# Letting the attention stage start inside the projection stage, with its first pass in two halves around the fold

## The reference

```python
def _L0_xattn_ref(q, k, v, Wq, bq, Wk, bk, Wv, bv, interference, amp, Wo, bo):
    ...
    def proj(x, W, bias):
        y = x @ W.T + bias
        y = y.reshape(b, s, H, dk, M)
        return jnp.transpose(y, (0, 2, 1, 3, 4))
    ...
    def interfere(x):
        return x + 0.1 * amp[0] * jnp.einsum('bhsdi,hij->bhsdj', x, interference)
    qh, kh, vh = (interfere(qh), interfere(kh), interfere(vh))
    scores = jnp.einsum('bhqdm,bhkdm->bhqkm', qh, kh) / math.sqrt(dk)
    weights = jax.nn.softmax(scores, axis=3)
    out = jnp.einsum('bhqkm,bhkdm->bhqdm', weights, vh)
    out = jnp.transpose(out, (0, 2, 1, 3, 4)).reshape(b, s, dm)
    return out @ Wo.T + bo
...
x = x + jnp.tanh(g_xattn[0]) * _L0_xattn_ref(_layernorm(x, axis=-1), ctx_4096, ctx_4096, ...)
x = x + jnp.tanh(g_ffn[0]) * _L0_ffn_ref(_layernorm(x, axis=-1), ...)
return x
```

## Time and profile before

| | |
|---|---|
| median of 3 runs | 1482.92 us (lowest 1480.61, highest 2315.33) |
| the profiled execution, its own time | 1477.51 us |
| its span in the trace | 1475.7 us |
| instructions | 22268 |
| TensorE busy | 1394.1 us, 94% of the span |
| VectorE, ScalarE, GpSimd busy | 673.8, 396.8, 234.3 us |
| mean granted TensorE clock | 0.972 |
| projections | until about 612 us of the span |
| attention | from 619.5 us to about 1070 us |
| feed-forward | from 1075.7 us to the end |

### The profile page before, as it was taken

One profiled execution on the slowest core, in us unless ns is written; L12 is line 12 of the kernel. 1 busy time (PEld: TensorE's weight loads), 2 busy tenths in 40 slices (PEclk: granted clock), 3 DMA queues, 4 the chain that ended last, 5 costly groups with the idle time before them and its releaser, 6 DMA issues. The chain is left out here.

```text
span 1475.7 us, 22268 instructions
## 1 busy us (share of the span) xinstructions
PE 1394.1 (94%) x8592; PEld 1153.3 (78%) x8592; DVE 673.8 (46%) x1377; ACT 396.8 (27%) x736; POOL 234.3 (16%) x400
## 2 busy tenths in 40 slices
PE   7999999999999999669999999999968999999998
PEld 6887887878888888457777777777756888888887
DVE  5322131231655544456666767676656424333211
ACT  3311111011212212224555555455424111110100
POOL 0000000000000000014555555555600000000000
PEclk9999999999999999858999999999979999999999
DMA  5763645536457777866777776776451211211101
GB/s 195 204 173 129 142 147 136 146 135 145 162 164 182 167 191 187 249 177 191 209 224 208 224 227 209 215 202 201 133 219 43 90 68 58 86 43 72 57 29 57
DMA packets 181719, 224.86 MB, mean 152 GB/s; under 512 B 24048, under 2 KB 122352, under 8 KB 181616
## 3 DMA queue, kind: packets, MB, share of 16 engines
q1 hardware_dynamic: 167792, 189.90, 44.3%
q10 hardware_dynamic: 13824, 33.56, 7.1%
HBM read 136.89 MB, written 85.46 MB: 151 GB/s over the span
## 5 line engine op out<-in xcount | busy, mean ns | idle before, releaser
L963 DVE TRANSPOSE_TENSOR_REDUCE part<-bank 128x16 f32<-128x512 f32 x256 | 167.7, 693 | 28.9 <-PE bank L837 26.8
L916 ACT ACTIVATE probT<-bank 128x512 f32<-128x512 f32 x256 | 138.6, 595 | 128.3 <-PE bank L868 128.3
L151 PE MATMUL bank<-place_a,w_hi 128*128 128x512 f32 x384 | 152.1, 396 | 7.9 <-DVE place_a L144 7.9
L495 DVE SCALAR_TENSOR_TENSOR stage_lo<-bank,bias_mixed,stage_hi 128x512 fp32r<-128x512 f32 x64 | 48.0, 751 | 240.1 <-ACT stage_hi L497 240.1
L153 PE MATMUL bank<-place_a,w_lo 128*128 128x512 f32 x384 | 150.5, 392 | 0.0
L152 PE MATMUL bank<-place_a,w_hi 128*128 128x512 f32 x384 | 150.0, 391 | 0.0
L497 ACT ACTIVATE stage_hi<-bank,bias_mixed 128x512 fp32r<-128x512 f32 x64 | 44.0, 688 | 268.1 <-PE bank L153 259.3
L816 PE MATMUL bank<-place_a,oT_hi 128*128 128x512 f32 x256 | 108.1, 422 | 0.3 <-POOL oT_lo L1042 0.3
L1236 DVE SCALAR_TENSOR_TENSOR v_place<-bank,gates,v_place 128x512 f32<-128x512 f32 x32 | 24.0, 751 | 175.1 <-PE bank L153 175.1
L151 PE MATMUL bank<-place_a,yT_hi 128*128 128x512 f32 x256 | 102.1, 399 | 1.5 <-DVE place_c L144 1.5
L151 PE MATMUL bank<-place_b,place_a 128*128 128x512 f32 x256 | 100.4, 392 | 1.4 <-DVE place_c L144 1.4
(11 more groups left out here) (179 smaller groups left out, 2698.4 us busy)
## 6 DMA issues: line engine op xcount, KB each, us to landing
q_in<-q_rows SPq DMA_DIRECT2D x212, 100.0 KB
k_in<-k_rows SPq DMA_DIRECT2D x84, 196.0 KB
k_rows<-stage_hi SPq DMA_DIRECT2D x128, 128.0 KB, 2.5
v_pad<-v_out SPq DMA_DIRECT2D x32, 512.0 KB, 2.7
q_rows<-stage_hi SPq DMA_DIRECT2D x128, 128.0 KB, 2.5
v_place<-v_pad ACTq DMA_DIRECT2D x32, 512.0 KB, 4.7
v_place<-x_mid SPq DMA_DIRECT2D x30, 512.0 KB, 3.6
k_rows<-stage_lo SPq DMA_DIRECT2D x64, 128.0 KB, 2.5
```

The source lines that it names most:

```text
L151: nc.tensor.matmul(bank_ap, sh, mh, start=(i == 0), stop=False)
L495: lambda bank: nc.vector.scalar_tensor_tensor(out=lo[:], in0=bank[:], scalar=bias, in1=hi[:].bitcast(F32), op0=ALU.add, op1=ALU.subtract),
L916: act.activation(probT[o % NPT][:, i].rearrange("k a p q -> k (a p q)"), two_bank[i][:], ACT.Exp).then_inc(s_exp, 1)
L963: dve.tensor_reduce(part[at][:, :, 2 * i:2 * i + 2, :].rearrange("k a p b -> k a (p b)"), one_bank[i][:].rearrange("k (a b t) -> k a b t", ...
```

## The change

The change has four parts.

- **One program part.** Projections and attention share one `nc.Block()`. Each engine goes on from its last projection job to its first attention slot without a barrier. `projected(eng)` makes SyncE and ScalarE wait at the start of their attention code for all projection jobs and all stores. TensorE waits for the bank that it is about to use; the banks' roles are numbered anew (`turn`), and the second half of a first pass gets the bank of the last query job.
- **Four octets loaded early.** Octets 0 to 3 get buffers of their own place in SBUF (`early_q`, `early_k`, where `mix`, `bv_row` and `v_out` lay) and are loaded during the last four query jobs. Two output-weight chunks now follow each of the query jobs 1 and 2, so that none is left at the end.
- **First pass in two halves.** `first_pass(o, 1)` fills the second bank, which no fold uses, and stands at the start of slot o. `first_pass(o, 0)` fills the first bank and stands at the end of slot o. The fold of octet s moves from slot s to slot s + 1, in the middle of the slot's work, and with it the maxima of octet s and GpSimd's two instructions. The second pass of octet s - 3 stands at the beginning of slot s, or right after the values and the fold.
- **SyncE.** In a slot `load_oct` now comes before `place_max`. The loads of the feed-forward's first x tiles are issued at other slots and wait for other semaphores.

```diff
-        with proj, ExitStack() as st, nc.Block() as block:
+        attend = top.enter_context(ExitStack())
+        block = attend.enter_context(nc.Block())
+        with proj, ExitStack() as st:
...
-                    elif c:
-                        wo_chunk(c - 1, free_places)
+                    elif 0 < c < KC - 1:
+                        for _ in range(2 if c < 3 else 1):
+                            wo_chunk(wo_next, free_places)
+                            wo_next += 1
...
+                    if g == NG - 1 and c >= KC - EARLY:
+
+                        def load_early(sp, o=c - (KC - EARLY)):
+                            sp.wait_ge(s_cleared, EARLY)
+                            sp.wait_ge(s_stage[o % 2], 96 * ((NG * KC + o) // 2 + 1))
+                            load_kq(sp, o, (first_k, second_k, early_k[2], early_k[3])[o],
+                                    early_q[o] if o else first_q, s_kq[o])
+                        plan.append((len(line.jobs) + 0.7, load_early))
...
+            def projected(eng):
+
+                eng.wait_ge(project_line.emptied, len(project_line.jobs))
                 for i in range(2):
-                    sp.wait_ge(s_stage[i], 96 * NG * KC)
-                    sp.wait_ge(s_vst[i], 16 * NB)
-            run_phase(block, line, plan, stores_end)
+                    eng.wait_ge(s_stage[i], 96 * NG * KC)
+                    eng.wait_ge(s_vst[i], 16 * NB)
...
-                for o in range(1, LAG):
-                    load_oct(o)
+                projected(sp)
                 for s in range(SLOTS):
+                    if EARLY <= s + LAG < OCTS:
+                        load_oct(s + LAG)
                     if 1 <= s <= OCTS:
                         place_max(s - 1)
-                    if s + LAG < OCTS:
-                        load_oct(s + LAG)
...
+                def first_pass(o, i):
+                    if o < OCTS:
+                        slot = o % KQ
+                        if i == 1:
+                            pe.wait_ge(s_kq[slot], 48 * (o // KQ + 1))
+                            if o:
+                                pe.wait_ge(s_part, 2 * o - 1)
+                        elif o:
+                            pe.wait_ge(s_max, o)
+                        if o == 0:
+                            pe.wait_ge(project_line.emptied, project_line.last_use(turn[i]))
+                        for p in (2 * i, 2 * i + 1):
+                            dst = one_bank[i][:].rearrange("k (a p q) -> k a p q", a=2, p=2)[:, :, p % 2, :]
+                            last = pe.matmul(dst, k_in[slot][:, p, :], q_in[slot][:, :, p, :], start=True, stop=True,
+                                             skip_group_check=True)
+                        last.then_inc(s_one, 1)
...
+                for s in range(SLOTS):
+                    work, h = proj_at(s), half_at(s, 0)
+                    first_pass(s, 1)
+                    if h is not None:
+                        values(h)
+                        fold(s - 1)
+                        second_pass(s - LAG)
+                    else:
+                        second_pass(s - LAG)
+                        for part_of in work[:1]:
+                            project(*part_of)
+                        fold(s - 1)
+                    for part_of in work[1:]:
                         project(*part_of)
+                    first_pass(s, 0)
```

More of the change, by code:

```diff
@@ L35, in bank, with last_use @@
         return self.banks[n % len(self.banks)]
+    def last_use(self, i):
+        return max(n for n, job in enumerate(self.jobs) if job.pe and n % len(self.banks) == i) + 1
     def wait_filled(self, eng, end):
@@ L167, in build @@
         first_k, second_k = (sb(n, [ROWS, 4, P], F32R) for n in ("first_k", "second_k"))
-        KQ = 6
+        with ExitStack() as overlaid:
+            mix = sb("mix", [P, KC, P], stack=overlaid)
+            bv_row = sb("bv_row", [P, D], stack=overlaid)
+            v_out = [sb(f"v_out{i}", [P, PAIRS // 2, 2, 32], F32, overlaid) for i in range(2)]
+        with ExitStack() as overlaid:
+            yin, raw_d = ([sb(f"{n}{i}", [P, D], F32, overlaid)[:] for i in range(2)] for n in ("yin", "raw_d"))
+        early_q = {i: sb(f"early_q{i}", [ROWS, 2, 4, P], F32R) for i in (2, 3, 1)}
+        early_k = {i: sb(f"early_k{i}", [ROWS, 4, P], F32R) for i in (2, 3)}
+        KQ, EARLY = 6, 4
         s_kq = [sem(f"s_kq{i}") for i in range(KQ)]
@@ L684, in build @@
         wo_hi, wo_lo = place_a, place_c
         dn_hi, dn_lo = (half_place(place_b, i, NE * R) for i in range(2))
-        v_place = [sb(f"v_place{i}", [P, 2 * D]) for i in range(2)]
         with ExitStack() as overlaid:
@@ L712, in build @@
             gated = sb("gated", [P, HALF], F32, st)
-            one_bank, two_bank, v_bank, o_bank = (banks[2 * i:2 * i + 2] for i in range(4))
+            turn = [(len(project_line.jobs) - 2 + i) % len(banks) for i in range(len(banks))]
+            one_bank, two_bank, v_bank, o_bank = ([banks[i] for i in turn[2 * j:2 * j + 2]] for j in range(4))
             norm = LayerNorm("c", st)
@@ L1001, in _ @@
                             stages[s - start](dve)
+                    if s < OCTS:
+                        partial_max(s, 0)
             @block.gpsimd
             def _(pool):
-                for i in range(2, KQ, 2):
-                    pool.memset(q_in[i][:].bitcast(F32), 0.0).then_inc(s_zero[0], 1)
+                project_line.wait_filled(pool, len(project_line.jobs))
+                for i in range(EARLY, KQ):
+                    pool.memset(q_in[i][:].bitcast(F32), 0.0).then_inc(s_zero[i % 2], 1)
                 def add_gated(b, out):
```

142 lines of the change are left out of this document (62 added, 80 removed).

## The result

The changed kernel takes a median of 1604.6 us (1597.95 to 1608.27 in 4 runs). Its ratio to the kernel before is 1.0824, with an interval of 1.0762 to 1.0886: 8% slower. Two of the four runs of the kernel before on that chip (2315.33 and 2784.32 us) lie far above the other two (1480.61 and 1482.92 us) and are left out of the ratio.

A forecast was written before the change was run, and what follows sets the result against it. The steady attention was taken as bound by TensorE (busy 303.74 of 313 us). From 1477.5 us: -4 at the junction, +65 and +1.6 for gaps, +44 for the clock, giving 1584 us; range 1505 to 1640.

The forecast's parts named there:

- case (C): The forecast itself: a gap in every steady period plus low clock after it, 1584 us; chance 0.42.
- the two value slots at the start: Value slots before product triples begin: give some 1.5 us of the junction's gain back through late maxima.
- The start of the attention: Junction: SyncE let go at about 623, first second pass near 632, a gain of 5.5 us.
- The junction's net: Junction gain less what the first two value slots give back: -4 us, bounds +1 and -12.
- The gap: Steady slots: TensorE waits 3.0 us a period for maxima two slots after the values; +65 us over 26 periods.
- Their 8 KB travel on the same queue as the 400 KB loads, and they land after the load ahead of them: SyncE's queue in the slots: maxima land after the load ahead of them, taken as 0.3 us behind it.
- The clock: Steady slots: 85 in 100 gaps bring a low-clock stretch costing 2.0 us; 1.7 us a period, +44 us.
- Rival B: Steady slots: the gap comes but the clock holds, giving 1540 us; chance 0.33.
- The period: Steady slots: TensorE's work 12.45 us, plus 3.0 of gap and 1.7 of clock, instead of 12.97.
- The exponentials' wait: Slot after a value slot: the second pass's second half waits 0.35 us for the exponentials, its cover gone.
- Rival A: Slots: maxima overtake the load, so no gap and no waits for keys; 1456 us, 1.5% faster; chance 0.12.
- The end of the attention and the feed-forward part: After the last first passes: x tiles loaded later still land in time, feed-forward untouched; no change in time.

The follow-up runs named there:

- e5: The junction's part of the change alone, on the kernel before: slots as before, maxima placed ahead of the load; 1472.17 us, ratio 0.9955.
- e2: The kernel before with SyncE's two steps exchanged, the load issued before the maxima; 1540.58 us, ratio 1.0414.
- e1: The changed kernel with SyncE's two steps in the old order, maxima placed before the load; 1509.49 us, ratio 1.0207 to the kernel before.
- e6: The changed kernel without the v tile loads after the first four, leaving out part of the computation; 1518.82 us, ratio 1.0275 to the kernel before.
- e4: The changed kernel with the maxima's DMA issued by GpSimd on its own queue; 1585.3 us, ratio 1.0716 to the kernel before.
- e3: The changed kernel with 13 filler matmuls of zeros before the late second pass; 1564.82 us, ratio 1.0577 to the kernel before.
- e8: e7 with a value slot's fold moved to between the two halves of the values; 1458.99 us, ratio 0.9862 to the kernel before.
- e7: e5 with a value slot's second pass ahead of the values and ScalarE's exponentials before its copy; 1466.74 us, ratio 0.9927 to the kernel before.

## Why the prediction came out as it did

The forecast, 1584 us and slower by more than 2%, named the right case (C) with the right mechanism of the gap and the clock; the measured 1604.6 lies in its range, 20 us above it. The step that failed is the sum's term for the two value slots at the start, put at 1.5 us where the trace has 7.1. By its steps:

- **The start of the attention.** Forecast: `projected` lets SyncE go at about 623 and the first second pass starts near 632. The trace: 621.44 (the bias row's issue) and 631.79. e5, which has the maxima first, gains 8.0 us at that point and 6.4 at the end, by the medians.
- **"The two value slots before the product triples begin give some 1.5 us back".** This is the term that was mis-sized: from octet 0 to octet 13 the changed kernel loses 7.1 us on the kernel before. The two gaps alone take 3.62 and 4.31 us, in the rows of 655.51 and 673.00, longer than the steady ones. The forecast's own sum would have given that: without the two triples of 0.69 us in TensorE's work, 7.25 - (4.07 - 1.38) = 4.6 us a gap, an estimate from its terms. The granted clock was low, too, for 27 us instead of 14 between 650 and 690. e2 loses 6.8 us in the same piece from the load-first order alone, and e1, without that order, 2.1. The junction's net was forecast at -4 us and came to +1.4 at octet 13.
- **The gap.** Forecast: 3.0 us once a period, in the slot two after the values, ended by the DMA of the maxima. The trace: 26 gaps there (octets 14 to 114), 2.1 to 4.1 us long, 3.06 in the mean. Its parts fit as well: from the load's issue to the second pass 6.62 us in the mean, forecast 6.10 + 0.3 + 0.1 = 6.5; between the two second passes 7.39, forecast 7.25; and TensorE's work in it 4.3, forecast 4.07. e1 and e2 show that SyncE's order makes the gap, and e6 that the v tile makes 2.2 us of the delay. One size was off: the last two periods, forecast at 1.6 us together because no v tile is loaded in them, had gaps of 1.4 and 2.7 us and cost 6.4 us.
- **"Their 8 KB travel on the same queue as the 400 KB loads, and they land after the load ahead of them".** The second half held; the reason that the first half suggests did not. In a value slot they land with the load on GpSimd's queue all the same (e4).
- **The clock.** Forecast: 85 in 100 gaps bring on a low stretch that costs 2.0 us, 44 us in all. The trace: 25 of the 26 gaps have a low stretch beside them, 21 of 3.4 us and four of 6.8 us, 99 us in all, of which half is lost: 49 us. So the share was too low and the price right. e3 gives back 40 us with the delay kept, some of it eaten by the filler. Rival B is refuted as a forecast; its price of 1540 lies 25 us under the 1565 of e3, whose clock held. Its argument, the gap of 1.84 us before 231 that did no harm, was weak: in the changed kernel's trace the gap at that same place (1.83 us, before 228) was followed by a low stretch, from 229.4, and the one before 139 was not.
- **The period.** Forecast: 12.45 + 3.0 + 1.7 = 17.15 us. Over the 26 periods it covers it was 17.44 (octet 13 to 117; before 12.97), of which 3.06 are gap and 1.90 clock; the 12.48 left bear out the 12.45, though the recorded parts of that number (up to 0.25 us gained, 0.35 of wait) don't add up to it. That the 17.19 of the table is so near to 17.15 is luck: it takes in the shorter periods at the end. The 26 periods lost 116.3 us against 65 + 44 = 109.
- **The exponentials' wait** of 0.35 us is there, a little smaller: the second pass of the slot after the values takes 0.90 us (908.82) instead of 0.63. The first passes wait for no keys, as forecast, and VectorE costs nothing in the steady slots.
- **Rival A** falls: in a value slot, with a load in flight, the maxima are waited for until 6 us after their issue and not 2.6. e8 comes near its price of 1456 with 1459, but by another order of the slots. Its premise that with the maxima in time the rest follows doesn't hold for this order: e1 has late loads and late maxima at once. I made the same mistake once more in what I expected of e1.
- **The end of the attention and the feed-forward part** lost 2.6 us, forecast as nothing; no run looked into it.

Together: 5.4 us at the junction, 7.3 in the 26 periods, 4.8 in the last two and 2.6 behind them are the 20 us by which the forecast was low.

The change, then, is a junction worth 6 us, a new order of TensorE's slots that costs 26 to 37, and an order of two DMAs that costs 95 of which some 40 are clock. What stays open: how the 26 to 37 us split up beyond the 15 us of waits for DMAs and the 7 of the exponentials, and whether the fold or the moved second pass makes them; and why the packets of a small DMA start late beside a large one of another queue.

## What to carry to other kernels

Where a small transfer that the next step waits for shares the DMA engines with a prefetch, count from the event that lets the prefetch go to the use of the small one, with the prefetch's full time in between, and count it in each slot that is short, the first ones too; here another queue for the small one did not save it. Issue the small one first, and free the prefetch's buffers earlier (e7 and e8) rather than let the prefetch overtake. In this kernel a TensorE gap of 3.1 us in every period cost 1.9 us more by the clock behind it, and gaps of about 1 us cost next to nothing more (e6), so shortening such a gap pays more than its own length. And where a mean per period comes out as forecast, look at the periods one by one before you call the forecast right.

## What the runs showed that was not expected

- **The price of the clock can be read inside one trace.** In e4 the gaps before 774.30 and 789.67 (1.7 and 2.7 us) brought no low stretch, and the periods that follow them take 15.4 and 15.0 us. From 805 to 1112, where each gap has one, a period takes 17.1 us in the mean.
- **Low stretches come evenly.** In the changed kernel's trace they begin at 690.2, 707.3, 724.4, 741.4, 758.5 and so on up to 1072.5, at distances of 17.07 us and twice 20.5, while single periods there take 16.3 to 19.1 us. There is one for each gap, and the mean distance (17.38 us) is the mean period of that piece (17.40), so the evenness doesn't show that gaps and clock keep step; why the distances are so equal was not tried.
- **Shorter gaps in every period left the clock nearly alone**: from 690 to 1100 three low stretches in e6 (waits of 1.1 us in the mean) and one in e1 (0.7 us), eleven in e2 (1.5 us), where 3 us brought one in nearly every period. The same length does not always do the same: in e4 2.65 us brought none (before 789.67) and 2.55 us one (before 821.53).
- **A small DMA can share a large one's fate across queues**: 2.1 to 2.7 us two slots after a value slot, 4.9 to 6.4 us in a value slot, 0.7 to 0.8 us behind a load of 400 KB and beside a v tile of 512 KB, both on other queues (e4).
